# GpSimd rounds the 4-bit weights with one add-add operation in place of two add-multiply operations

## The chip, the cores and the metric

The kernel runs on one core of a Trainium2 chip. The metric is the device time of one execution in microseconds; for a change it is the median over the runs of a kernel. All stages of the program run in this one core, on five engines that have a queue of instructions each: TensorE (PE), VectorE (DVE), ScalarE (ACT), GpSimd (POOL) and SyncE (SP, which issues nearly all of the transfers).

## The reference

A cross-attention block is followed by a feed-forward block whose weights and activations are quantised. `x` is (2, 2048, 512), the context (2, 128, 512), the gate and up weights (1536, 512) and the down weight (512, 1536).

```
x = x + xattn(layernorm(x), ctx, Wq, Wkv)      # softmax attention over 128 context rows
h = act_qdq(layernorm(x))                      # 16 bits, one scale from the largest |h|
up   = act_qdq(h @ lpbq_dequant(w_up).T)
gate = act_qdq(h @ lpbq_dequant(w_gate).T)
sig  = round(sigmoid(gate) * 65536) / 65536
o    = act_qdq(act_qdq(gate * sig) * up)
x    = x + o @ lpbq_dequant(w_down).T

def lpbq_dequant(w):                           # blocks of 32 inputs
    s  = max(max|w over the block| / 7, 1e-12)
    return clip(round(w / s), -8, 7) * s
```

Each `act_qdq` needs the maximum over the whole tensor before any of it can be rounded, which cuts the program into stages. The change is in `round(w / s)` of `lpbq_dequant`.

## The kernel before, in words

The 4096 tokens are 8 groups of 4 tiles of 128 tokens. The program is written engine by engine: each engine's instructions stand in a fixed order written out by hand, and the engines meet at semaphores. No scheduler reorders anything.

Stage 1 is the attention with the second layer norm. TensorE turns the tiles of `x`, computes scores and the product with the values (L743, L804, L818). VectorE adds the residual (`residual`, L1361), forms the negated mean (`mean2`, L1366), once per group the variance (`var2`, L1371, which raises `ve2_d`), and takes the largest |h| of pairs of tiles (`h_max`, L1382). ScalarE sums the squares (`spread`, L1038). GpSimd has two jobs here, in one queue. It computes reciprocal roots and normalises the groups 0 to 6 (`rstd1`, L672 and L675; `normalise`, L704 and four times L707), and between these it dequantises the gate weights in 8 pieces (`quant_weights`, L691 to L697). The weights lie in `WN`, 128 partitions with 6144 float32 each, so that a piece is 128 x 768.

`quant_weights` multiplies a piece by the inverse scales of its blocks, adds the constant 12582912 and takes it off again, which leaves the nearest integer in float32, and multiplies by the scales. Each step waits for the one before by a semaphore. At the end of stage 1 VectorE reduces the maxima to one column (L1449), GpSimd takes the maximum over the partitions (`all_max(1)`, a `partition_all_reduce`, L683), VectorE makes the scale of it (L1285, L1443, L1444), ScalarE rounds h (L1096), VectorE splits it into two float16 parts (L1458, L1460), and the gate product starts (L871).

The order at the end of stage 1 on GpSimd is this part of the program:

```
            for g in range(NG - 1):
                normalise(g)
                if g < 4:
                    rstd1(g + 4)
                if g < 5:
                    quant_weights(g + 3, NBLK // 8, 0)
            all_max(1, "hmx", "hall")
```

`normalise(6)` raises the power of group 6 and of group 7 one after the other (two times L704, each behind its own `ve2_d`) and then scales the four tiles of group 6. Group 7 is normalised by ScalarE.

Stage 2 is the gate product, 8 groups of 6 units of 24 matmuls on TensorE. Under it GpSimd dequantises the up weights (8 pieces) and then the down weights (8 pieces). ScalarE splits each into float16 parts at fixed units of the gate product (`natural_hi`, behind `w_deq`), VectorE forms the rest (`natural_lo`), and SP turns them by transposing transfers. Stage 3 is the up product with the sigmoid work beside it, stage 4 the rounding of the up product and a first part of the down product, stage 5 the down product. GpSimd has only one `all_max` at each border there.

Of the kernel before, what the change touches and what calls it, by code (L numbers as in the profile page):

```python
# [44 lines left out]
ROUND = 12582912.0  # L45
# [90 lines left out]
ALU = mybir.AluOpType  # L136
# [12 lines left out]
def build(nc, x, ctx_in, wq_in, wkv_in, wg_in, wu_in, wd_in, out):  # L149
# [10 lines left out]
    with ExitStack() as stack:  # L160
        def sem(name):
            return stack.enter_context(nc.semaphore(name))
# [155 lines left out]
        w_blk, w_inv, w_rnd, w_deq = sem("w_blk"), sem("w_inv"), sem("w_rnd"), sem("w_deq")  # L318
# [345 lines left out]
        @block.gpsimd  # L664
        def _(pool):
            pool.wait_ge(consts, 5)

            def rstd1(g):

                r = rs1[:, TI * g:TI * g + TI]  # L670
                pool.wait_ge(ve1_d, g + 1)
                nc.gpsimd.tensor_tensor(r, ve1[:, TI * g:TI * g + TI], half[:, TI * g:TI * g + TI],  # L672
                                        ALU.pow).then_inc(rs1_d, 1)
                pool.wait_ge(rs1_d, 2 * g + 1)
                nc.gpsimd.tensor_scalar(r, r, SCALE, 1.0, ALU.mult, ALU.mult).then_inc(rs1_d, 1)  # L675

            for g in range(2):
                rstd1(g)

            def all_max(k, src, dst):  # L680

                pool.wait_ge(col_max, k + 1)
                nc.gpsimd.partition_all_reduce(col[dst], col[src], P, RMAX).then_inc(col_all, 1)  # L683

            def quant_weights(at, blocks, base):

                w = WN[:, bass.ds(at * blocks * BLK, blocks * BLK)]
                wb = w.rearrange("p (n e) -> p n e", e=BLK)
                inv = binv[:, bass.ds(at * blocks, blocks)].unsqueeze(2).to_broadcast([P, blocks, BLK])
                scl = bscl[:, bass.ds(at * blocks, blocks)].unsqueeze(2).to_broadcast([P, blocks, BLK])  # L690
                nc.gpsimd.tensor_tensor(wb, wb, inv, ALU.mult).then_inc(w_inv, 1)  # L691
                pool.wait_ge(w_inv, base + at + 1)
                nc.gpsimd.tensor_scalar(w, w, ROUND, 1.0, ALU.add, ALU.mult).then_inc(w_rnd, 1)
                pool.wait_ge(w_rnd, 2 * base + 2 * at + 1)
                nc.gpsimd.tensor_scalar(w, w, -ROUND, 1.0, ALU.add, ALU.mult).then_inc(w_rnd, 1)
                pool.wait_ge(w_rnd, 2 * base + 2 * at + 2)
                nc.gpsimd.tensor_tensor(wb, wb, scl, ALU.mult).then_inc(w_deq, 1)  # L697

            def normalise(g):

                for r in (g, g + 1) if g + 2 == NG else (g,):
                    c = bass.ds(TI * r, TI)
                    pool.wait_ge(ve2_d, r + 1)
                    nc.gpsimd.tensor_tensor(rs2[:, c], ve[:, c], half[:, c], ALU.pow).then_inc(rs2_d, 1)  # L704
                pool.wait_ge(rs2_d, g + 1)
                for i in range(TI):
                    nc.gpsimd.tensor_scalar(H[:, g, i], X[:, g, i], negm[:, bass.ds(TI * g + i, 1)],  # L707
                                            rs2[:, bass.ds(TI * g + i, 1)], ALU.add, ALU.mult).then_inc(h2_d, 1)

            all_max(0, "wmx0", "wall0")  # L710
            pool.wait_ge(w_blk, 1)
            quant_weights(0, NBLK // 8, 0)
            rstd1(2)
            for at in (1, 2):
                quant_weights(at, NBLK // 8, 0)
            rstd1(3)
# [8 lines that stand above are left out]
            all_max(2, "wmx1", "wall1")  # L725
            pool.wait_ge(w_blk, 2)
            for at in range(8):
                quant_weights(at, NBLK // 8, 8)
            all_max(3, "wmx2", "wall2")
            pool.wait_ge(w_blk, 3)  # L730
            for at in range(8):
                quant_weights(at, NBLK // 8, 16)

            all_max(4, "gmx", "gall")
            all_max(5, "smx", "sall")
            all_max(6, "umx", "uall")
            all_max(7, "omx", "oall")
# [973 lines left out]
```

## Time and profile before

| | |
|---|---|
| times of the runs shown | 901.20, 902.86, 903.91 us |
| median | 902.86 us |
| span of the profiled execution | 898.3 us |
| median less span | 4.56 us |
| PE busy | 865.5 us, 96% |
| DVE busy | 651.1 us, 72% |
| ACT busy | 560.2 us, 62% |
| POOL busy | 157.4 us, 18%, 160 instructions |
| DMA | 230.20 MB, mean 256 GB/s |

The profiled execution's own time is not recorded beside its span. The span runs from its first to its last instruction, and the 4.56 us are what the median of the runs has on top of it. The three runs lie 2.7 us apart. A busy share is an average over all stages: GpSimd works nearly without a break in the second half of stage 1 and in two stretches under the gate product, and hardly at all behind these.

### The profile page before, as it was taken

To read this page: it belongs to the slowest core of one execution; us is meant where nothing else is said; L and a number is where in the kernel's file an instruction comes from. 1 tells how busy PE (TensorE), PEld (TensorE's weight loads), DVE (VectorE), ACT (ScalarE), POOL (GpSimd) and SP (SyncE) were. 2 spreads that over 40 slices of the span, in tenths; PEclk is the share of its full clock that TensorE was granted. 3 is DMA by queue.
4 is the path that set the end of the run, shared out by engine and by line. 5 is a ranking of instruction groups with operands and counts; after the bars stand their busy time and mean duration, and the time that the engine had idled before them with its cause. 6 is when DMAs were issued, how large, how long until landed. Compare 5 with 4: busy or idle time off the path is not lost.

```text
span 898.3 us, 11791 instructions
## 1 busy us (share of the span) xinstructions
PE 865.5 (96%) x4144; PEld 426.7 (47%) x4144; DVE 651.1 (72%) x918; ACT 560.2 (62%) x673; POOL 157.4 (18%) x160
## 2 busy tenths in 40 slices
PE   7999969999999999999999989999799989999998
PEld 5777544444444444444444434444344434444443
DVE  4879883754346243279997859856999997999892
ACT  2378875553553454489997859763789975555430
POOL 0099940089001950000000000000000000000000
PEclk9999989999999999999999999999999999999999
DMA  9822319775369649884339993799998897989872
GB/s 347 332 93 98 128 59 305 205 194 198 140 234 296 206 161 294 322 319 157 132 149 327 363 347 142 251 402 373 374 379 265 276 322 271 386 286 406 317 294 100
DMA packets 107548, 230.20 MB, mean 256 GB/s; under 512 B 47216, under 2 KB 47216, under 8 KB 105328
## 3 DMA queue, kind: packets, MB, share of 16 engines
q1 hardware_dynamic: 106352, 225.48, 70.8%
q10 hardware_dynamic: 1152, 4.19, 1.3%
q8 instruction: 21, 0.34, 0.2%
q14 instruction: 23, 0.19, 0.1%
HBM read 127.40 MB, written 92.27 MB: 245 GB/s over the span
## 4 chain that ended last, share of the span: by engine, by line
PE 66%; DVE 16%; issue 8%; DMA 6%; ACT 3%; SPq 0%; POOL 0%; DVEq 0%; ACTq 0%
PE ps L871 28%; PE ps L948 13%; PE ps L903 10%; PE ps L975 3%; DVE big L1596 3%; PE ps L804 3%; DVE big L1589 3%; PE ps L743 2%; PE ps L818 2%; DVE small L1523 2%; DMA big<-gate_park 2%; DMA product_park<-big 2%; DVE small L1511 2%; DVE big L1518 1%; PE ps L965 1%
## 5 line engine op out<-in xcount | busy, mean ns | idle before, releaser
L993 ACT ACTIVATE big<-ps 128x1024 f32<-128x1024 f32 (+2 forms) x166 | 138.7, 845 | 189.6 <-PE ps L871 102.8
L871 PE MATMUL ps<-big 128*128 (+1 forms) x1152 | 250.5, 381 | 2.3 <-DVE big L1460 2.3
L903 PE MATMUL ps<-big 128*128 (+1 forms) x1152 | 249.0, 379 | 2.3 <-ACT big L993 2.3
L871 PEld LDWEIGHTS ps<-big 128*128 128x128 f16 x1152 | 113.1, 98 | 139.4 <-issue 4.6
L903 PEld LDWEIGHTS ps<-big 128*128 128x128 f16 x1152 | 112.6, 98 | 138.5 <-issue 2.8
L1478 DVE TENSOR_REDUCE small<-big 128x1 f32<-128x1024 f32 x48 | 58.3, 1219 | 135.2 <-ACT big L993 135.1
L948 PE MATMUL ps<-big 128*128 128x512 f16 x576 | 125.1, 379 | 2.7 <-DVE big L1617 2.7
L683 POOL PARTITION_ALL_REDUCE small<-small x8 | 3.3, 410 | 509.3 <-DVE small L1558 181.5
L948 PEld LDWEIGHTS ps<-big 128*128 128x128 f16 x576 | 56.2, 98 | 71.1 <-issue 2.9
L929 PE MATMUL ps<-big 128*128 128x512 f16 x384 | 85.2, 383 | 4.5 <-ACT big L1223 4.5
L1529 DVE CUSTOM_DVE_ANT_0 big<-big,small 128x1024 f32<-128x1024 int16 x48 | 61.7, 1284 | 7.3 <-ACT big L1173 0.5
L1252 ACT ACTIVATE big<-big,small 128x1024 int16<-128x1024 f32 x48 | 53.2, 1136 | 16.7 <-DMA big<-up_park 16.5
L929 PEld LDWEIGHTS ps<-big 128*128 128x128 f16 x384 | 37.4, 99 | 52.0 <-issue 5.5
L1511 DVE TENSOR_REDUCE small<-big 128x1 f32<-128x1024 f32 x48 | 58.0, 1214 | 3.4 <-ACT big L993 3.4
L1258 ACT ACTIVATE big<-big 128x1024 f16<-128x1024 int16 x24 | 25.3, 1055 | 53.0 <-DVE big L1611 53.0
L1181 ACT ACTIVATE big<-big,small 128x1024 f32<-128x1024 int16 x48 | 55.1, 1149 | 4.6 <-ACT big L1173 0.4
L1173 ACT ACTIVATE big<-big,small 128x1024 int16<-128x1024 f32 x48 | 54.5, 1136 | 2.4 <-DMA big<-gate_park 2.4
L1216 ACT ACTIVATE big<-big,small 128x1024 int16<-128x1024 f32 x48 | 52.3, 1135 | 5.7 <-DVE small L1444 2.9
L1138 ACT ACTIVATE big<-big 128x1024 int16<-128x1024 f32 x48 | 50.5, 1052 | 6.9 <-DMA sign_park<-big 5.9
L743 PE MATMUL ps<-small,big 128*128 128x128 f32 x248 | 37.9, 294 | 12.8 <-DVE big L1389 5.1
L743 PEld LDWEIGHTS ps<-small,big 128*128 128x128 f32 x248 | 32.2, 153 | 28.6 <-issue 18.4
L691 POOL TENSOR_TENSOR big<-big,small 128x768 f32<-128x768 f32 x24 | 36.5, 1521 | 22.0 <-issue 21.6
(101 smaller groups left out, 1008.9 us busy)
## 6 DMA issues: line engine op xcount, KB each, us to landing
big<-up_park SPq DMA_DIRECT2D x90, 512.0 KB, 6.5
up_park<-big SPq DMA_DIRECT2D x48, 512.0 KB, 3.9
gate_park<-big SPq DMA_DIRECT2D x42, 512.0 KB, 2.9
big<-gate_park SPq DMA_DIRECT2D x42, 512.0 KB, 5.7
sign_park<-big SPq DMA_DIRECT2D x48, 256.0 KB, 3.1
big<-in_x_dram SPq DMA_DIRECT2D x8, 1024.0 KB, 17.5
x_park<-big SPq DMA_DIRECT2D x8, 1024.0 KB, 3.9
product_park<-big SPq DMA_DIRECT2D x16, 512.0 KB, 5.8
```

The costliest lines, as they stand in the source:

```text
L743: return nc.tensor.transpose(dst, src, ident)
L871: mm = nc.tensor.matmul(ps[:, 2 * (n % 2) + j], w[:, a, k, o:o + P], XT[:, g, b, k], start=(k == 0 and a + b == 0), stop=(k == KC - 1 and ...
L903: mm = nc.tensor.matmul(ps[:, b + j], WU[:, a, k, o:o + P], XT[:, g, c, k], start=(k == 0 and a + c == 0), stop=(k == KC - 1 and c == 1))
L929: mm = nc.tensor.matmul(ps[:, b0 + i], halves[:, PART[t], c * 512 + i * P:c * 512 + i * P + P], WD[:, b, 2 * n + c], start=(n == 0 and c + ...
L948: mm = nc.tensor.matmul(ps[:, i], o, WD[:, b, 2 * n + c], start=(n == 0 and c + a + b == 0), stop=(n == UPG - 1 and c + a == 2))
L993: return nc.scalar.activation(dst, src, ACT.Copy)
L1173: nc.scalar.activation(g_abs[:, i % 2], place(i), ACT.Abs, scale=col["ginv"]).then_inc(abs_d, 1)
L1181: nc.scalar.activation(place(i), g_int[:, i % 2], ACT.Sigmoid, scale=col["gsc"]).then_inc(sig_d, 1)
L1252: nc.scalar.activation(r_int[:, m % 4], ring(m), ACT.Copy, scale=col["uinv"]).then_inc(uq_d, 1)
L1478: nc.vector.tensor_reduce(gcol[:, bass.ds(g * UPG + n, 1)], shelf[:, SHELF[n]] if kept else gate_out[:, n % 2], AX.X, ALU.max, apply_absol ...
L1511: nc.vector.tensor_reduce(ucol[:, n:n + 1], up_place(n), AX.X, ALU.max, apply_absolute_value=True).then_inc(u_mx, 1)
L1529: nc.vector.tensor_tensor_reduce(place(i), g_abs[:, s], s_int[:, s], 1.0, scol[:, s:s + 1], ALU.mult, ALU.max, scol[:, s:s + 1]).then_inc( ...
```

## The change

The add and the subtraction of the rounding constant become the two arithmetic steps of one GpSimd instruction. The multiplication by 1.0, which was the second step of each of the two instructions, is gone, and so is one wait. The semaphore `w_rnd` is raised once for a piece and no longer twice, and the waits on it count accordingly. Line numbers behind the edit fall by 2.

```diff
                 nc.gpsimd.tensor_tensor(wb, wb, inv, ALU.mult).then_inc(w_inv, 1)
                 pool.wait_ge(w_inv, base + at + 1)
-                nc.gpsimd.tensor_scalar(w, w, ROUND, 1.0, ALU.add, ALU.mult).then_inc(w_rnd, 1)
-                pool.wait_ge(w_rnd, 2 * base + 2 * at + 1)
-                nc.gpsimd.tensor_scalar(w, w, -ROUND, 1.0, ALU.add, ALU.mult).then_inc(w_rnd, 1)
-                pool.wait_ge(w_rnd, 2 * base + 2 * at + 2)
+                nc.gpsimd.tensor_scalar(w, w, ROUND, -ROUND, ALU.add, ALU.add).then_inc(w_rnd, 1)
+                pool.wait_ge(w_rnd, base + at + 1)
                 nc.gpsimd.tensor_tensor(wb, wb, scl, ALU.mult).then_inc(w_deq, 1)
```

GpSimd's queue before, from the last piece of the gate weights to the maximum over the partitions (the first L704 and L707 are `normalise(5)`, then come `normalise(6)` and `all_max(1)`):

```order
L691 TENSOR_TENSOR big<-big,small 128x768
L693 TENSOR_SCALAR big<-big 128x768
L695 TENSOR_SCALAR big<-big 128x768
L697 TENSOR_TENSOR big<-big,small 128x768
L704 TENSOR_TENSOR small<-small 128x4
L707 TENSOR_SCALAR big<-big,small 128x512 x4
L704 TENSOR_TENSOR small<-small 128x4 x2
L707 TENSOR_SCALAR big<-big,small 128x512 x4
L683 ISA
```

The same place of GpSimd's queue in the changed kernel:

```order
L691 TENSOR_TENSOR big<-big,small 128x768
L693 TENSOR_SCALAR big<-big 128x768
L695 TENSOR_TENSOR big<-big,small 128x768
L702 TENSOR_TENSOR small<-small 128x4
L705 TENSOR_SCALAR big<-big,small 128x512 x4
L702 TENSOR_TENSOR small<-small 128x4 x2
L705 TENSOR_SCALAR big<-big,small 128x512 x4
L683 ISA
```

One instruction has gone from the piece, and nothing has changed its place. This stands 24 times in the program, 8 times in each of the three weights. The row of kind ISA is the one that makes GpSimd ready for `partition_all_reduce`.

VectorE's queue at the end of stage 1 is the same in both kernels apart from its line numbers (here those of before: L1371 is `var2`, L1382 `h_max`, L1389 the low part of the gate weights, L1449 the last maximum):

```order
L1371 TENSOR_SCALAR small<-small 128x4
L1382 TENSOR_REDUCE small<-big 128x1 x4
L1389 TENSOR_TENSOR big<-ps,big 128x4x128 x3
L1382 TENSOR_REDUCE small<-big 128x1
L1389 TENSOR_TENSOR big<-ps,big 128x4x128
L1382 TENSOR_REDUCE small<-big 128x1
L1389 TENSOR_TENSOR big<-ps,big 128x4x128
L1448 TENSOR_TENSOR small<-small 128x4
L1449 TENSOR_REDUCE small<-small 128x1
```

No instruction of VectorE, TensorE, ScalarE or SP is added, removed or moved.

## Rows read from the trace of the kernel before

**Rows 1.** Chain that ended last: start us, us, engine, output, line.

```profile
125.43 0.18 DVE small L1449
125.61 1.64 issue
127.25 0.39 POOL small L683
...
130.14 250.50 PE ps L871 x1152
```

**Rows 2.** Window of stage 1: busy us of PE, PEld, DVE, ACT, POOL; clock, DMA, GB/s.

```profile
33.00:101.00 68.00, 67.03 (x463) 54.05 (x464) 57.00 (x163) 51.75 (x144) 53.61 (x60) 1.00 0.30 125
```

**Rows 3.** Groups of GpSimd's instructions by line and form: busy us, mean ns, idle before.

```profile
L697 POOL TENSOR_TENSOR big<-big,small 128x768 f32<-128x768 f32 x24 | 37.6, 1565 | 2.0
L695 POOL TENSOR_SCALAR big<-big 128x768 f32<-128x768 f32 x24 | 21.6, 898 | 2.0
```

**Rows 4.** Timeline of GpSimd in stage 1: start us, us, instruction.

```profile
52.42 0.83 POOL L693 TENSOR_SCALAR big<-big 128x768 f32<-128x768 f32 x1
53.34 0.83 POOL L695 TENSOR_SCALAR big<-big 128x768 f32<-128x768 f32 x1
...
55.69 1.48 POOL L691 TENSOR_TENSOR big<-big,small 128x768 f32<-128x768 f32 x1
...
61.92 1.02 POOL L704 TENSOR_TENSOR small<-small 128x4 f32<-128x4 f32 x1
...
103.35 1.03 POOL L704 TENSOR_TENSOR small<-small 128x4 f32<-128x4 f32 x1
...
112.34 1.01 POOL L704 TENSOR_TENSOR small<-small 128x4 f32<-128x4 f32 x1
...
116.46 1.99 POOL L704 TENSOR_TENSOR small<-small 128x4 f32<-128x4 f32 x2
118.43 3.04 POOL L707 TENSOR_SCALAR big<-big,small 128x512 f32<-128x512 f32 x4
```

**Rows 5.** GpSimd's reconfiguration for L683, two stretches: ns min/median/max, first and last start.

```profile
L683 POOLq MODIFY_POOL_CONFIG  x2: 11/11/11, 31.0 to 31.1; - x2
...
L683 POOLq MODIFY_POOL_CONFIG  x2: 28/28/28, 121.6 to 121.7; - x2
```

**Rows 6.** Timelines of VectorE and GpSimd around two other partition maxima.

```profile
37.17 0.38 POOL L683 PARTITION_ALL_REDUCE small<-small  x1 [6.43 <-issue]
...
382.98 0.20 DVE L1503 TENSOR_REDUCE small<-small 128x1 f32<-128x48 f32 x1
383.32 0.38 POOL L683 PARTITION_ALL_REDUCE small<-small  x1 [56.53 <-DVE small L1503]
```

**Rows 7.** Timeline of VectorE in stage 1, the group variances of both layer norms.

```profile
55.78 1.42 DVE L1339 TENSOR_SCALAR small<-small 128x4 f32<-128x4 f32 x1
...
60.89 0.16 DVE L1371 TENSOR_SCALAR small<-small 128x4 f32<-128x4 f32 x1
...
80.47 0.68 DVE L1371 TENSOR_SCALAR small<-small 128x4 f32<-128x4 f32 x1
...
106.47 0.33 DVE L1371 TENSOR_SCALAR small<-small 128x4 f32<-128x4 f32 x1
...
115.92 0.60 DVE L1371 TENSOR_SCALAR small<-small 128x4 f32<-128x4 f32 x1
```

**Rows 8.** TensorE before the gate product, then windows at its start (clock third from last).

```profile
125.94 1.95 PE L889 MATMUL ps<-small 128*128 128x128 f32 x16
...
130.50:131.00 0.50, 0.50 (x4) 0.26 (x2) 0.47 (x3) 0.50 (x2) 0.00 (x0) 0.72 0.00 0
131.00:131.50 0.50, 0.50 (x3) 0.15 (x1) 0.50 (x2) 0.50 (x1) 0.00 (x0) 0.50 0.00 0
...
134.00:134.50 0.50, 0.50 (x4) 0.18 (x2) 0.50 (x2) 0.50 (x2) 0.00 (x0) 0.87 0.00 0
```

**Rows 9.** Timeline of ScalarE under the gate product, its wait for GpSimd's weights.

```profile
326.82 1.67 ACT L993 ACTIVATE big<-big 128x512 f16<-128x512 f32 x3 [2.10 <-POOL big L697]
```

## The prediction

> **What bounds the kernel now.** I read the chain that ended last first, because the edit touches only GpSimd, which is busy 18% of the span, and the question is whether any of its work lies on that chain. From 130.14 us TensorE's gate product is one uninterrupted piece of 250.50 us [rows 1], and before it, from 33 to 101 us, TensorE is busy 67.03 of 68.00 us [rows 2]. The edit's 24 places fall into three stretches: eight in stage 1, sixteen under the gate product. So the second look went to the gap between 101 and 130 us. There the chain runs over VectorE until L1449, then shows 1.64 us of "issue", and then GpSimd's L683 at 127.25 [rows 1]. This 1.64 us is the important row. The same step at 383.32 starts 0.14 us after VectorE's last maximum has ended (382.98 + 0.20) [rows 6]. So at 127.25 something other than VectorE's result was late.
>
> It is GpSimd itself. Its reconfiguration for L683 stands at 121.6 us, right behind its last scaling, which ends at 118.43 + 3.04 = 121.47 [rows 4, 5], and L683 comes 5.6 us later. In the first case of the trace the reconfiguration is at 31.0 and L683 at 37.17, 6.1 us later [rows 5, 6]. At 383.32 GpSimd had been idle for 56.53 us and L683 came at once. I read this as a fixed time of about 5.8 us from the end of GpSimd's ordinary work to its first partition maximum; where it is not yet over, it and not the maximum sets the start. The Trainium skill (GPSIMD Engine Reference, section 2.1 Instruction dispatch) says that the first call into freshly loaded GpSimd code pays about 6 us without an instruction in the profile. By its 5.95 us L683 would come at 127.4, by the rows at 127.25; the trace agrees, and the sum goes by the rows. So GpSimd's end of stage 1 is on the critical path after all, although no wait of another engine names it.
>
> **The change, part by part.** One instruction goes from each piece. From L693 to L695 it is 53.34 − 52.42 = 0.92 us, instruction and gap [rows 4]. The merged instruction is not in the trace. Its nearest row is the add-multiply on the same piece, 0.83 us alone [rows 4]; the far bound is the two-input operation on the same piece, 1.565 us on average [rows 3]. Both steps are plain arithmetic with constants in both forms, so I take 0.83. The saving is then 0.92 us for a piece, 7.4 us in each of the three stretches, and 0.92 − 0.73 = 0.19 us for a piece, 1.5 us in a stretch, at the far bound.
>
> *Under the gate product* sixteen pieces save 14.7 us of GpSimd's time and nothing of the span. The only wait for them is ScalarE's at 326.82, 2.10 us long [rows 9]. It will vanish, but ScalarE is not what TensorE waits for there: the gate product has no gap [rows 1]. Without that cover the wait would be worth 2.1 us at most. Whatever starts earlier behind it, the turning transfers of the down weights by some tenths, also ends under the gate product.
>
> *In stage 1* the eight pieces cannot hand on their 7.4 us, since between them GpSimd waits for VectorE's variances (L1371). `normalise(0)` starts at 61.92 and its variance is there at 60.89 + 0.16 = 61.05 [rows 4, 7], so after three pieces, 2.8 us earlier, it starts at about 61.1: 0.8 us are kept and the rest turns into a wait. Four rounds of `normalise`, `rstd1` and a piece take (103.35 − 61.92) / 4 = 10.36 us each [rows 4], and 9.44 after the change. The third begins at 61.1 + 2 x 9.44 = 80.0, but its variance is there only at about 80.47 + 0.16 = 80.63 [rows 7]. Then 80.7, 90.1, 99.6, and the short last round of 112.34 − 103.35 = 8.99, now 8.07, ends at about 107.7 [rows 4]. `normalise(5)` then starts some 4.6 us earlier than at 112.34. This lead is lost too: `normalise(6)` raises two powers, and the second needs the variance of group 7, which VectorE gives at 115.92 + 0.60 = 116.52 [rows 7]. Before, the two powers started at 116.46 and took 1.99 us [rows 4], so the second started at about 117.45, 0.9 us after its variance was there. What is left to gain on GpSimd is this 0.9 us, plus or minus what the variance itself moves.
>
> And it moves, because VectorE's small L1371 is held up by GpSimd. It takes 0.16 us when free, but 0.68, 0.33 and 0.60 us in the other rows, and the like instruction at 55.78 took 1.42 us; that one ended at 57.20, just when GpSimd's L691, started at 55.69, had ended at 57.17 [rows 4, 7]. The last one ended at 116.52, when GpSimd's scaling made way for the powers of 116.46. The Trainium skill (SBUF — State Buffer, section Who interferes with whom) has the rule: VectorE in a two-port mode and GpSimd exclude each other for a whole instruction, and the one that starts second waits. The trace agrees. After the change two of these matter, since from 101 us on VectorE works with hardly a break. At 115.92 GpSimd will stand idle and wait for that very result, so L1371 takes 0.16: 0.44 us gained. At 106.47 GpSimd should just be starting the last two-input operation of the last piece (107.7 − 1.48 = 106.2, or some tenths later): if it is first, VectorE waits until about 107.9, 1.1 us later than the 106.80 of before; if VectorE is first, it gains 0.17. The two instructions start within 0.3 us of each other, and I can't tell which wins.
>
> *The sum.* Where VectorE loses at 106.47, the last variance comes at 116.52 + 1.1 − 0.44 = 117.2, GpSimd ends at 117.2 + 1.0 + 3.04 = 121.25 instead of 121.47, and L683 gains 0.2 us. Where it wins, the variance comes at 115.9, GpSimd ends at 120.0, and L683 gains 1.5 us. VectorE's own maximum (125.61) would come 0.66 later or 0.61 earlier and is no limit in either case, because it has 1.64 − 0.14 = 1.5 us of slack [rows 1, 6]. With the far bound for the merged instruction the gain on GpSimd lies inside the same 0.2 to 1.5. I take the middle, 0.9 us. Against the profiled execution that is a span of 898.3 − 0.9 = 897.4; with the 4.56 us that the median has on top, 902.0 us. A measurement of this kernel can tell about 0.3%, 2.7 us, from no change; this lies well within.
>
> **The rivals.** *As above: about 902.0, own range 901.3 to 902.7.* Chance 0.68.
>
> *Nothing at all, 902.9.* Either L683 follows VectorE's last maximum at a fixed distance, or a merged instruction costs as much as two did, so that the change does not do what it says. For the first speaks that the chain names VectorE before the 1.64 us; against it speak the 0.14 us of 383.32. Chance 0.11.
>
> *Faster, 899.7 to 900.3.* At the start of the gate product TensorE's granted clock falls to 0.50, its level of 1.2 GHz, from about 130.7 to 134.1 [rows 8], after it had had no work from 127.9 to 130.14 [rows 1, 8]. In that stretch 0.5 x 3.4 = 1.7 us are lost. The change shortens this idle time from 2.2 to some 1.4 us, and the fall may then be left out: 902.0 − 1.7 = 900.3, or 899.7 with the full 1.5 us. Against it: a pause of 1.4 us remains, and half the idle time need not decide it. Chance 0.13.
>
> *Slower, about 903.5.* The held-up L1371 at 106.47, if VectorE's end and not GpSimd's readiness sets L683: then the 1.1 − 0.44 = 0.66 us go straight into the span. It decides from the point at which VectorE is later than before by more than its 1.5 us of slack, or at once if that slack is not real. For it speaks the exclusion just shown, which the change moves to new places; by the skill's rule alone, with a second collision of up to 1.48 us behind the first, 904.3 could come out. Against it: both later L1371 then meet an idle GpSimd. Chance 0.08.
>
> **How the numbers follow.** The likeliest case gives 902.0. The range has to take in the faster case at 899.8 and the slower at 904.0, and with them the spread of 901.2 to 903.9 in the runs shown, which is wider than the effect. Faster by over 0.3% needs the full gain and the clock's 1.7 us together: 0.1. Slower by over 0.3% needs more than any one mechanism gives: 0.05. The rest, 0.85, is no change that can be told.
>
> **What the profile will show.** Right: the merged instruction at 0.83 us; GpSimd about 22 us less busy (24 x 0.92); new idle times of GpSimd before L702 that name VectorE's variance, the last of them before the second power of `normalise(6)`; L683 again 5.6 to 5.8 us behind GpSimd's last scaling, and at 125.8 to 127.1; no wait of ScalarE for the down weights at 326; the gate product in one piece. Wrong: L683 1.64 us behind L1449 again whatever GpSimd does; an L1371 of more than 1 us that pushes L1449 beyond 127; a merged instruction above 1.3 us; a gap in the gate product.

## The result and the profile after

| | before | after |
|---|---|---|
| median | 903.55 us (5 runs, 901.20 to 904.60) | 919.89 us (5 runs, 917.17 to 922.40) |
| ratio to before | | 1.0189, 95% interval 1.0167 to 1.0210 |
| span of the profiled execution | 898.3 us | 919.3 us (its own time 921.28) |

The kernel became slower by 1.9% by the ratio of the runs, and the medians lie 16.3 us apart, where no measurable change was forecast. The groups of the changed kernel's GpSimd instructions, by line and form (busy us, mean ns, idle before), are the counterpart of [rows 3] and give the reason in one row:

```profile
L693 POOL TENSOR_SCALAR big<-big 128x768 f32<-128x768 f32 x24 | 68.0, 2831 | 2.2
...
L695 POOL TENSOR_TENSOR big<-big,small 128x768 f32<-128x768 f32 x24 | 35.6, 1484 | 2.0
L705 POOL TENSOR_SCALAR big<-big,small 128x512 f32<-128x512 f32 x28 | 21.1, 767 | 0.7
```

L693 is the merged instruction. It takes 2.83 us on average, not 0.83, and so it takes more than the two that it replaces. In the kernel before, the first of these two has this row in the same view (the second, L695, is in [rows 3]):

```profile
L693 POOL TENSOR_SCALAR big<-big 128x768 f32<-128x768 f32 x24 | 20.3, 847 | 2.2
```

Twenty-four merged instructions are busy for 68.0 us, against 20.3 + 21.6 = 41.9 us before.

The timeline of the changed kernel's GpSimd at the end of stage 1 is to be read beside [rows 4]; the two rows behind it are VectorE's last maximum and the first row of the gate product in the timelines of those engines:

```profile
115.77 2.79 POOL L693 TENSOR_SCALAR big<-big 128x768 f32<-128x768 f32 x1
118.64 1.48 POOL L695 TENSOR_TENSOR big<-big,small 128x768 f32<-128x768 f32 x1
120.08 1.03 POOL L702 TENSOR_TENSOR small<-small 128x4 f32<-128x4 f32 x1
...
124.19 1.98 POOL L702 TENSOR_TENSOR small<-small 128x4 f32<-128x4 f32 x2
126.17 3.01 POOL L705 TENSOR_SCALAR big<-big,small 128x512 f32<-128x512 f32 x4
135.51 0.38 POOL L683 PARTITION_ALL_REDUCE small<-small  x1 [6.33 <-issue]
...
131.64 0.17 DVE L1447 TENSOR_REDUCE small<-small 128x1 f32<-128x18 f32 x1
...
138.40 11.85 PE L869 MATMUL ps<-big 128*128 128x512 f16 x41 [4.30 <-DVE big L1458]
```

GpSimd's ordinary work ends at 126.17 + 3.01 = 129.18, not at 121.47 as in [rows 4], 7.7 us later. L683 follows at 135.51, although VectorE's last maximum has been there since 131.81. The gate product starts at 138.40, 8.26 us later than in [rows 1].

Under the gate product the timelines of ScalarE and TensorE show the second loss. The first row is the counterpart of [rows 9]:

```profile
344.60 1.67 ACT L991 ACTIVATE big<-big 128x512 f16<-128x512 f32 x3 [10.47 <-POOL big L695]
...
348.17 49.17 PE L869 MATMUL ps<-big 128*128 x216 [4.75 <-ACT big L991]
397.18 5.13 PE L901 MATMUL ps<-big 128*128 128x512 f16 x23
```

ScalarE waits 10.47 us for the down weights, in place of 2.10. While it waits in its queue it cannot evacuate the next unit of the gate product (copy its result out of the memory that TensorE writes to), and TensorE stands still for 4.75 us, from 343.42 to 348.17. Windows of half a microsecond have TensorE's granted clock at 0.50, the lower of its levels (1.2 GHz), from 345.6 to 352.4, so behind the pause for some 4 us more. In two wider windows (busy us of PE, PEld, DVE, ACT, POOL, then clock, DMA, GB/s):

```profile
343.00:345.00 2.00, 0.42 (x2) 0.00 (x0) 0.00 (x0) 0.40 (x1) 1.48 (x2) 1.00 0.00 0
345.00:352.00 7.00, 3.83 (x10) 1.32 (x11) 5.35 (x8) 7.00 (x12) 0.00 (x0) 0.54 0.36 137
```

The profile's page has the gate product as one group:

```profile
L869 PE MATMUL ps<-big 128*128 (+1 forms) x1152 | 254.1, 385 | 9.2 <-ACT big L991 4.7 <-DVE big L1458 4.3
```

The same 1152 matmuls take 254.1 us, 3.6 more than the 250.50 of [rows 1], and the stretches at the lower clock account for nearly all of it. There are two. Behind the stall it is 348.17 to 352.4, where half of 4.2 us is lost, 2.1 us. The other is at the start of the gate product, where the clock is at 0.50 until 144.2, for 5.8 us, which costs 2.9 us in place of the 1.7 us of before; these 1.2 us belong to the loss of stage 1. With the stall that is 3.6 + 4.75 = 8.4 us, and the timelines agree: from 138.40 to 397.18 are 258.8 us, from 130.14 to the first matmul of the up product before, at 380.47, 250.3. Up to the end of the gate product the two executions are thus 8.3 + 8.4 = 16.7 us apart.

The medians are 16.3 us apart, but the two profiled spans 21.0 us. The other 4.3 us lie behind the gate product, which took 522.1 us after and 517.8 before. Over the eight kernels of this study that run the whole program it lies between 517.8 and 523.2 us, and the highest value is that of `p_up`, whose median is that of the kernel before. So I read no effect from it. The profiled execution of the kernel before is shorter than most: in all executions with both numbers the time is 1.8 to 2.9 us above the span, mostly 1.9, so that of the 4.56 us that were added to its span ahead of the prediction some 2.7 are the distance of that one execution from the median. Single executions differ by some microseconds in other parts too, so that the agreement of 16.7 with 16.3 is closer than these numbers can promise.

### The profile page after: what moved, and what is told of

Its sections match the earlier page's. It is cut to its first block, busy times and chain, and to the rows that moved or that the text cites. A ratio compares the mean times of both kernels' runs of the same rounds, so it can differ in the third digit from the quotient of the medians.

```text
span 919.3 us, 11767 instructions
## 1 busy us (share of the span) xinstructions
PE 875.1 (95%) x4144; PEld 429.1 (47%) x4144; DVE 652.1 (71%) x918; ACT 560.1 (61%) x673; POOL 180.9 (20%) x136
## 2 busy tenths in 40 slices
DMA packets 107548, 230.20 MB, mean 250 GB/s; under 512 B 47216, under 2 KB 47216, under 8 KB 105328
## 3 DMA queue, kind: packets, MB, share of 16 engines
q10 hardware_dynamic: 1152, 4.19, 1.2%
## 4 chain that ended last, share of the span: by engine, by line
PE 35%; issue 18%; DMA 14%; DVE 13%; POOL 12%; ACT 5%; SPq 2%; DVEq 0%; POOLq 0%; ACTq 0%
PE ps L869 16%; PE ps L946 14%; POOL big L693 5%; PE ps L973 3%; DVE small L1509 3%; DMA big<-product_park 3%; POOL big L695 2%; DVE small L1521 2%; POOL big L691 2%; DMA big<-in_L_ffn_w_gate_dram 2%; DMA big<-gate_park 2%; DMA product_park<-big 2%; DMA up_park<-big 2%; POOL big L705 1%; DVE big L1516 1%
## 5 line engine op out<-in xcount | busy, mean ns | idle before, releaser
L869 PE MATMUL ps<-big 128*128 (+1 forms) x1152 | 254.1, 385 | 9.2 <-ACT big L991 4.7
L901 PE MATMUL ps<-big 128*128 (+1 forms) x1152 | 250.7, 381 | 3.1 <-ACT big L991 3.1
L683 POOL PARTITION_ALL_REDUCE small<-small x8 | 3.3, 410 | 507.7 <-DVE small L1556 182.3
L693 POOL TENSOR_SCALAR big<-big 128x768 f32<-128x768 f32 x24 | 68.0, 2831 | 2.2
```

The costliest lines, as they stand in the source:

```text
L693: nc.gpsimd.tensor_scalar(w, w, ROUND, -ROUND, ALU.add, ALU.add).then_inc(w_rnd, 1)
L869: mm = nc.tensor.matmul(ps[:, 2 * (n % 2) + j], w[:, a, k, o:o + P], XT[:, g, b, k], start=(k == 0 and a + b == 0), stop=(k == KC - 1 and ...
L901: mm = nc.tensor.matmul(ps[:, b + j], WU[:, a, k, o:o + P], XT[:, g, c, k], start=(k == 0 and a + c == 0), stop=(k == KC - 1 and c == 1))
```

## The experiments

In each edit below the kernel before is the base. Ratios are to runs of the kernel before on the same chip.

### Pairs of steps, alone: `m_forms`

The kernel copies x and leaves the computation out; GpSimd runs eleven pairs of steps, each three times, then VectorE two. One of the blocks reads:

```
for w in (768, 768, 384):
    nc.gpsimd.tensor_scalar(dst[:, 0:w], src[:, 0:w], ROUND, -ROUND, ALU.add, ALU.add)
```

> This kernel leaves out the whole computation: it copies x to the output and runs GpSimd's two-step operation alone, nothing beside it, on 128 x 768 (twice) and 128 x 384 float32, with eleven pairs of steps, and two pairs on VectorE behind it. Theory 'the pair': add-add is slow in itself, so add-add takes 2.8 us here too and about 1.4 us on 384, add-multiply 0.83 us, whatever the constants are; every pair whose second step is a multiplication is near 0.83. Rival 'the place': the merged instruction is held up in the kernel by VectorE, so that here, alone, it takes 0.83 us like the others. Rival 'the constants': add-add with 0.0 as second constant takes 0.83 and only the one with the large negative constant 2.8.

Its groups by line and form (busy us, mean ns, idle before):

```profile
L77 POOL TENSOR_SCALAR dst<-src 128x768 f32<-128x768 f32 x2 | 5.6, 2782 | 0.2
L101 POOL TENSOR_SCALAR dst<-src 128x768 f32<-128x768 f32 x2 | 5.6, 2781 | 0.2
L85 POOL TENSOR_SCALAR dst<-src 128x768 f32<-128x768 f32 x2 | 5.6, 2780 | 0.2
L109 POOL TENSOR_SCALAR dst<-src 128x768 f32<-128x768 f32 x2 | 5.6, 2780 | 0.2
...
L113 POOL TENSOR_SCALAR dst<-src 128x768 f32<-128x768 f32 x2 | 5.5, 2772 | 0.2
...
L89 POOL TENSOR_SCALAR dst<-src 128x768 f32<-128x768 f32 x2 | 1.7, 832 | 0.2
L97 POOL TENSOR_SCALAR dst<-src 128x768 f32<-128x768 f32 x2 | 1.7, 831 | 0.2
L73 POOL TENSOR_SCALAR dst<-src 128x768 f32<-128x768 f32 x2 | 1.7, 830 | 22.3 <-DMA src<-in_x_dram 22.2
L93 POOL TENSOR_SCALAR dst<-src 128x768 f32<-128x768 f32 x2 | 1.7, 830 | 0.2
...
L77 POOL TENSOR_SCALAR dst<-src 128x384 f32<-128x384 f32 x1 | 1.5, 1495 | 0.1
...
L125 DVE TENSOR_SCALAR dst<-src 128x768 f32<-128x768 f32 x2 | 1.1, 560 | 85.3 <-POOL dst L116 85.3
L129 DVE TENSOR_SCALAR dst<-src 128x768 f32<-128x768 f32 x2 | 1.1, 560 | 0.1
L73 POOL TENSOR_SCALAR dst<-src 128x384 f32<-128x384 f32 x1 | 0.5, 511 | 0.1
```

All eleven pairs on 128 x 768, from this view:

| pair | line | us |
|---|---|---|
| add, multiply (by 1.0 or by 0.5) | L73, L97 | 0.83 |
| multiply, add | L89 | 0.83 |
| multiply, multiply | L93 | 0.83 |
| add, add (second constant −12582912 or 0.0) | L77, L109 | 2.78 |
| add, subtract; subtract, add | L81, L85 | 2.78 |
| subtract, multiply | L101 | 2.78 |
| add, max; max, min | L105, L113 | 2.78, 2.77 |

The place and the constants are out as causes: with nothing beside it, and with 0.0 as the second constant too, add-add takes 2.78 us, nearly the 2.83 us of the kernel. The part of the expectation that every pair with a multiplication behind is fast fell as well: subtract-multiply is slow. The eleven pairs have two durations and nothing between them. From 384 to 768 elements the fast pairs take (830 − 511) / 384 = 0.83 ns for each element in a partition, the other pairs (2782 − 1495) / 384 = 3.35 ns, four times as much; the fixed part is about 0.2 us in both. VectorE takes 0.56 us for add-multiply and for add-add alike.

### The merged instruction in one weight at a time: `p_stage1`, `p_up`, `p_down`

The edit in short, with `lo` and `hi` for the numbers of each kernel; the waits between the steps and the raising of `w_rnd` are left out, here and in the edits below:

```diff
-                nc.gpsimd.tensor_scalar(w, w, ROUND, 1.0, ALU.add, ALU.mult)
-                nc.gpsimd.tensor_scalar(w, w, -ROUND, 1.0, ALU.add, ALU.mult)
+                if lo <= base + at < hi:      # 0 to 8, 8 to 16, 16 to 24
+                    nc.gpsimd.tensor_scalar(w, w, ROUND, -ROUND, ALU.add, ALU.add)
+                else:
+                    (the two as before)
```

> The merged instruction in the eight pieces of the gate weights alone. Theory 'GpSimd late at two places': the gate product starts about 8.2 us later (130.14 to 138.4), and nothing is added behind it: about 911.8 us, ratio near 1.009. Rival 'it is all stage 1, the rest follows from it': 919 us.

> The merged instruction in the eight pieces of the up weights alone. Both theories: GpSimd ends them some 8.4 us later, at about 235, ScalarE's first split of them waits some 3 us, TensorE does not: 903 us, within 0.3%. If it is slower by more, the cost under the gate product is not only that of the down weights.

> The merged instruction in the eight pieces of the down weights alone. Theory 'GpSimd late at two places': GpSimd ends at about 335 instead of 327, ScalarE's evacuation of the next unit comes late, the gate product has a stall of about 4 us and a stretch of half clock behind it, and the parked transfers shift: 908 to 913 us. Rival 'it is all stage 1': 903 us, because these pieces have cover.

| | median | ratio, 95% interval |
|---|---|---|
| `p_stage1`, gate weights | 912.59 us | 1.0118 (1.0089 to 1.0146) |
| `p_up`, up weights | 902.17 us | 0.9986 (0.9966 to 1.0006) |
| `p_down`, down weights | 910.82 us | 1.0100 (1.0063 to 1.0136) |

The medians of the first and the third lie 10.2 and 8.4 us above the 902.4 of the kernel before; together 18.6, against 16.3 in the changed kernel, which the intervals allow. Neither loss is a result of the other. In `p_stage1` the later start of the gate product (138.43) accounts for 8.3 of the 10.2 us, and 0.7 us more is in the gate product, which starts with 5 us at the lower clock; the rest is within the interval. The chain that ended last has the whole gate product in one piece, only later:

```profile
138.43 251.24 PE ps L877 x1152
```

In `p_up` the timeline of GpSimd has the eight pieces from 181.37 to 230.20, 48.8 us, and before from 183.05 to 226.68, 43.6. That is 5.2 us longer and not 8.3, because more of GpSimd's instructions ran over their usual time in this stretch before (L697 took up to 2.33 us, not 1.48) than now. They end at 230.20, not at the 235 expected. ScalarE's first split waits 0.68 us for them, less than the 3 us expected, and TensorE's gate product is uninterrupted (248.80 us): the same instruction, and no cost. In `p_down` GpSimd ends the down weights at 332.95, 2 us before the 335 expected, and the timelines of ScalarE and TensorE show:

```profile
332.98 1.67 ACT L999 ACTIVATE big<-big 128x512 f16<-128x512 f32 x3 [9.89 <-POOL big L703]
...
336.56 49.19 PE L877 MATMUL ps<-big 128*128 x216 [4.17 <-ACT big L999]
```

The stall and the stretch at the lower clock came as expected: the clock is at 0.50 from 334.4 to 341.2, which costs 2.3 us behind the stall. That is 6.5 us of the 8.4 between the medians, whose interval begins at 5.7.

### Another instruction of nearly the same length: `p_third`

```diff
                 nc.gpsimd.tensor_scalar(w, w, -ROUND, 1.0, ALU.add, ALU.mult)
+                nc.gpsimd.tensor_scalar(w, w, 0.0, 1.0, ALU.add, ALU.mult)
```

> The kernel before with a third rounding instruction behind the two in every piece, which adds 0.0 and multiplies by 1.0 (a fast pair). A piece then takes 0.92 us more than before, against 1.04 us more with add-add. Theory 'only the time of GpSimd counts': the same two delays at nearly the same size, the gate product starts about 7.3 us later and stalls by some 3 us: 916 to 919 us, ratio 1.014 to 1.018. Rival 'add-add does something else beyond its duration' (to VectorE, or to the clock): clearly less, below 912.

918.68 us, ratio 1.0182 (1.0153 to 1.0211). The two-instruction rounding with a third fast one behind costs as much as the merged one, as far as the intervals can tell. So the time that GpSimd needs is enough to explain the loss, and no other effect of add-add is seen. The timelines have L683 at 134.46, 5.91 us behind GpSimd's last scaling, the gate product at 137.36, the wait for the down weights at 8.82 us, and TensorE's stall at 3.1 us. In the profiled execution, the fastest of four, the gate product ends 12.4 us later than before, while the medians are 16.1 us apart. The rows of one execution give a loss only to within some microseconds.

### The premise made true: `p_short`

```diff
-                nc.gpsimd.tensor_scalar(w, w, ROUND, 1.0, ALU.add, ALU.mult)
-                nc.gpsimd.tensor_scalar(w, w, -ROUND, 1.0, ALU.add, ALU.mult)
+                nc.gpsimd.tensor_scalar(w, w, 0.0, 1.0, ALU.add, ALU.mult)
```

> One instruction for the rounding that takes what the prediction took for the merged one: it adds 0.0 and multiplies by 1.0, 0.83 us. It leaves the rounding of the weights out. Theory (the sum of the prediction, with its premise made true): L683 comes 0.2 to 1.5 us earlier, 901 to 902.5 us, ratio 0.998 to 1.000. Rival 'GpSimd's 7.4 us count in full': 895 us.

902.50 us, ratio 0.9989 (0.9970 to 1.0008). The timeline of its GpSimd at the end of stage 1:

```profile
109.30 3.01 POOL L705 TENSOR_SCALAR big<-big,small 128x512 f32<-128x512 f32 x4
112.72 1.01 POOL L702 TENSOR_TENSOR small<-small 128x4 f32<-128x4 f32 x1 [0.41 <-DVE small L1369]
116.06 1.01 POOL L702 TENSOR_TENSOR small<-small 128x4 f32<-128x4 f32 x1 [2.34 <-DVE small L1369]
117.07 3.01 POOL L705 TENSOR_SCALAR big<-big,small 128x512 f32<-128x512 f32 x4
125.87 0.38 POOL L683 PARTITION_ALL_REDUCE small<-small  x1 [5.79 <-DVE small L1447]
```

With an instruction of the assumed 0.83 us the forecast holds for GpSimd row by row. GpSimd waits for the variance of group 7, ends at 120.08, and L683 comes at 125.87, 1.4 us earlier than in [rows 1]. ScalarE's wait for the down weights is gone, and the gate product is in one piece.

From L683 on the forecast does not hold. It let L683's gain through to the span. Here the gate product starts at 129.66 in the timeline (129.87 in the chain), only 0.5 us earlier than before, and the chain that ended last no longer names GpSimd but TensorE's own sixteen matmuls in front of it (L887, which is L889 of [rows 8]):

```profile
126.45 3.41 PE ps L887 x16
129.87 248.88 PE ps L869 x1152
```

They take 3.62 us in the timeline in place of 1.95, because the granted clock is at 0.50 in this stretch, and 1.00 in the kernel before. These are the windows of `p_short`:

```profile
124.00:127.50 3.50, 2.87 (x14) 2.50 (x13) 3.19 (x10) 1.48 (x4) 0.38 (x1) 0.50 0.00 0
127.50:130.00 2.50, 2.50 (x13) 2.25 (x12) 1.72 (x6) 2.50 (x5) 0.00 (x0) 0.50 0.00 0
130.50:134.00 3.50, 3.50 (x18) 1.57 (x16) 3.50 (x7) 3.50 (x5) 0.00 (x0) 1.00 0.02 5
```

The lower clock is then over where the gate product begins, which takes 1.6 us less. By its end the execution is 1.9 us ahead. The whole is within 0.3%. So a merged rounding that were really fast would be worth about 0.1% here by the ratio of the runs, less than one can tell.

### The change of GpSimd's work, alone: `m_switch`

The computation is left out; GpSimd runs add-multiply (M) and partition maxima (R) behind one another:

```
M M R R R M M R M
```

> This kernel leaves out the whole computation: it copies x to the output and runs on GpSimd alone two add-multiply instructions, three partition maxima, two add-multiply, one maximum, one add-multiply, each behind the one before. Theory 'changing between ordinary work and the maximum costs a fixed time': 5.6 to 6.3 us before the first and the fourth maximum, some 7 us before the add-multiply behind a maximum, and well under 0.5 us before the second and third maximum. Rival 'the maximum itself is slow to start': the same gap before all four.

```profile
23.53 0.83 POOL L74 TENSOR_SCALAR dst<-src 128x768 f32<-128x768 f32 x1
30.00 0.38 POOL L76 PARTITION_ALL_REDUCE dst<-src  x1 [5.64 <-issue]
30.48 0.35 POOL L78 PARTITION_ALL_REDUCE dst<-src  x1
30.93 0.35 POOL L80 PARTITION_ALL_REDUCE dst<-src  x1
38.05 0.83 POOL L82 TENSOR_SCALAR dst<-src 128x768 f32<-128x768 f32 x1 [6.77 <-issue]
38.96 0.83 POOL L84 TENSOR_SCALAR dst<-src 128x768 f32<-128x768 f32 x1
45.53 0.38 POOL L86 PARTITION_ALL_REDUCE dst<-src  x1 [5.74 <-issue]
52.65 0.82 POOL L88 TENSOR_SCALAR dst<-src 128x768 f32<-128x768 f32 x1 [6.74 <-issue]
```

The timeline shows 5.64 and 5.74 us before a maximum behind ordinary work, 0.1 us between maxima, and 6.77 and 6.74 us on the way back. The time belongs to the change and not to the maximum.

### How much delay the gate product hides: `p_down3`

```diff
+                if 21 <= base + at < 24:
+                    nc.gpsimd.tensor_scalar(w, w, ROUND, -ROUND, ALU.add, ALU.add)
+                else:
+                    (the two as before)
```

> The merged instruction in the last three of the eight pieces of the down weights alone. In the runs so far TensorE's stall in the gate product is ScalarE's wait for the down weights less 5.7 us (8.82 and 3.1, 9.89 and 4.2, 10.47 and 4.75), and before it was 2.10 and nothing. Theory 'a reserve of 5.7 us': with 3 x 1.04 us more the wait is about 5.2 us, TensorE has no stall in the gate product, about 903 us, within 0.3%. Rival 'each piece costs its share': 3/8 of the 8.4 us that all eight cost, 905.8 us.

904.07 us, ratio 1.0027 (1.0010 to 1.0044). The times do not decide: they are within the theory's 0.3%, and the rival's three eighths of 8.4 us, 3.2 us, are within the interval of 0.9 to 4.0 us too. The trace has neither of the two as stated. In the timelines of ScalarE and TensorE:

```profile
329.03 1.67 ACT L999 ACTIVATE big<-big 128x512 f16<-128x512 f32 x3 [4.66 <-POOL big L703]
...
359.69 1.02 ACT L999 ACTIVATE big<-ps 128x1024 f32<-128x1024 f32 x1 [8.33 <-DMA big<-big]
...
375.14 1.06 ACT L1144 ACTIVATE big<-big 128x1024 int16<-128x1024 f32 x1 [7.96 <-DMA sign_park<-big]
...
360.77 15.71 PE L877 MATMUL ps<-big 128*128 x72 [1.20 <-ACT big L999]
377.17 5.35 PE L877 MATMUL ps<-big 128*128 x24 [0.68 <-ACT big L999]
```

At the first place the reserve is there: a wait of 4.66 us and no stall. But the delay goes on to the transposing transfers of the down weights, for whose end ScalarE waits before it evacuates the first unit of the last group. That wait is 8.33 us now, 5.32 before, and there TensorE's reserve is smaller. It stalls for 1.20 us. It stalls for 0.68 us again three units later, where ScalarE comes late because it waits 7.96 us for a store of signs to memory (`sign_park`) to free its buffer. The stalls' 1.9 us are most of the 2.2 us between the medians.

## Why the prediction was wrong

**The step that failed** is the price of the merged instruction: "Both steps are plain arithmetic with constants in both forms, so I take 0.83." It takes 2.78 us alone and 2.83 us in the kernel, and lies outside the bound of 1.565 us that was set above it. Shown by `m_forms`: the duration depends on the pair of steps, and add-add is not among the fast pairs. The row of L693 in the profile before was one of a fast pair and said nothing of another. The Trainium skill (GPSIMD Engine Reference, section 3.1 Elementwise — side-by-side cycle accounting) has 1.03 cycles for each element in a body of up to two operations. The fast pairs agree with it at 0.83 ns, 1.0 cycle of its 1.2 GHz; the other pairs, at 3.35 ns, do not, and the measurement decides.

**The far bound** was therefore no bound. It was taken from the two-input operation as the costliest row on the same piece. The sign of the effect hung on the bound: with 2 x 0.92 = 1.84 us for two instructions and their gaps, the break-even of the merged one is 1.75 us. "A merged instruction costs as much as two did" was a rival at 902.9; that it could cost more was no case at all. Two of the signs of being wrong that the prediction named did appear, a merged instruction above 1.3 us and a gap in the gate product, but none of its four cases had a price for them.

**Stage 1: mechanism right, sign of the term wrong.** The prediction put GpSimd's end, plus some 5.8 us of change to L683, on the critical path. The fixed time held in every kernel: L683 comes 5.79 us behind GpSimd's last scaling in `p_short`, 5.91 in `p_third`, 6.33 in the changed kernel, there 3.7 us after VectorE's maximum was ready, and `m_switch` shows the change alone. That the critical path runs through it holds for every delay here, but not for the gain: in `p_short` only 0.5 us of L683's 1.4 reached the start of the gate product, because TensorE's own L887 ended last. The waits on the variances limit only a gain. A delay finds no reserve: a piece has 2.79 us and a gap of 0.09 in place of 1.84, 1.04 us more, eight pieces 8.3 us; L691 starts 0.45 us earlier in this execution (44.12, 44.57 before), and GpSimd ends 7.7 us later. With 0.55 us more for the change that is the 8.26 us of the gate product. Another 1.2 us were lost behind its start, by a longer stretch at the lower clock.

**Under the gate product: cover right for a gain, too small for this loss.** "The only wait for them is ScalarE's at 326.82", worth nothing when it vanishes, was read correctly, and in `p_short` the wait is gone and nothing is won by it. But a wait of 2.10 us that is there already is the place where a delay enters. From 8.82, 9.89 and 10.47 us of this wait TensorE's stalls were 3.1, 4.17 and 4.75: about 5.7 us are hidden at the first place, and by `p_down3` less at the second. The up weights ended 3.5 us later in `p_up`, with no wait before and one of 0.68 us now, and cost nothing.

**The held-up variance.** That L1371 would be held up at 106.47 with some chance was right in kind. In `p_short`, whose GpSimd runs as the prediction had it, the instruction starts at 105.95 and takes 0.74 us, between the two cases that were worked out. It ends at 106.69, when GpSimd's add-multiply L693 (105.83 to 106.66) has ended, and not a two-input operation as had been supposed. In the changed kernel it is 1.48 us at 108.67, but VectorE's maximum was not what was waited for, so that it cost nothing there.

**The clock.** The faster case rested on the fall of the granted clock at the start of the gate product being left out. The chain of `p_short` has the gate product in 248.88 us, 1.6 us less than [rows 1], and `p_up` in 248.80, with nothing of the change in stage 1. In both, and in `p_down`, the clock is at 0.50 in front of the gate product, from 121 us or earlier, and at 1.00 by 130.5; before and in `p_down3` it has risen by 124 and falls again at about 130.6. There TensorE had paused for 2.3 us in front of the gate product, in the other three for at most 0.6, since L889 ran slowly into it. So this varies between executions with no change of stage 1, and the 1.6 us need not be the change's. The saving that this case had counted does occur, but with slower matmuls ahead of it, which it had not counted.

**The range.** It was drawn a little narrower than its own cases, whose ends are 899.7 and 904.3 us where the range has 899.8 and 904.0. At 919.9 us measured it made no difference.

## What to carry to other kernels

On GpSimd, fusing two steps into one instruction is a gain only if the pair is a fast one. Measure the new pair alone before counting instructions: the row of another pair is no price, and two fast instructions can be cheaper than one slow one (here 1.84 against 2.88 us, with their gaps). When an engine's queue has a wait at its end, ask for both directions, since waits that swallow a gain do not give any reserve against a loss. And where an unknown duration decides the sign, set its upper bound by the point of break-even, not by the costliest row at hand.

## What the runs showed of the hardware that was not expected

- GpSimd's two-step operation with constants on float32 has two speeds: 0.83 ns for each element in a partition for add-multiply, multiply-add and multiply-multiply, 3.35 ns for add-add, add-subtract, subtract-add, subtract-multiply, add-max and max-min. The values of the constants that were tried (1.0 or 0.5; −12582912 or 0.0) have no effect. Why the pairs part there is not shown.
- VectorE shows no such difference between add-multiply and add-add: 0.56 us for both pairs that were run on 128 x 768.
- The change from ordinary work to `partition_all_reduce` on GpSimd costs 5.6 to 6.4 us (6.43 at 37.17 us in [rows 6]) and the way back 6.7 us or more, also when nothing else runs.
